# The first loads of a four-layer kernel in five pieces on two queues, with eight small products ahead of them

## The reference, cut to what matters

```
def _dense(x, wi, wo):
    return jax.nn.relu(x @ wi) @ wo
s0 = _dense(hidden_states, share_wi[0], share_wo[0])
...
out = expert_out * g[:, 0, None, None] + s0 * g[:, 1, None, None] + s1 * g[:, 2, None, None] + s2 * g[:, 3, None, None]
```

## Time and profile before

| what | us |
|---|---|
| runs: median of 3 (lowest, highest) | 1641.2 (1638.75, 1642.07) |
| the profiled execution, its own time | 1641.15 |
| its span in the profile | 1639.3 |
| TensorE busy in the span | 1606.8 (98%) |
| TensorE's first matmul starts | 8.78 |
| TensorE's first matmul on `sum` (down 0) starts | 15.02 |

### The profile page before, as it was taken

How to read it: one execution, slowest core, us unless ns; L and a number is a source line. 1 busy time by engine, 2 the same in 40 slices (tenths; PEclk the granted TensorE clock), 3 DMA queues, 4 the chain that set the end, 5 groups by cost and what they waited for, 6 DMA issues and landing times.

```text
span 1639.3 us, 22537 instructions
## 1 busy us (share of the span) xinstructions
PE 1606.8 (98%) x7980; PEld 1360.5 (83%) x7980; DVE 1106.7 (68%) x1710; ACT 861.0 (53%) x1530; POOL 480.7 (29%) x420
## 2 busy tenths in 40 slices
PE   7999999999989999999999999999999999999998
PEld 6898898898977888888888888888888888877887
DVE  5665565465767876776776776776876786666556
ACT  5543343344546666656665665665665665643332
POOL 2121121124733541341431431441440440130000
PEclk9999999999989999999999999999999999999998
DMA  6522131131320010010010010000000010030000
GB/s 207 193 81 75 52 104 51 51 103 52 116 78 26 14 39 27 14 39 26 14 39 26 16 37 27 26 26 26 26 26 26 26 39 14 26 90 17 14 14 26
DMA packets 28460, 79.06 MB, mean 48 GB/s; under 512 B 4790, under 2 KB 9526, under 8 KB 28230
## 3 DMA queue, kind: packets, MB, share of 16 engines
q1 hardware_dynamic: 28054, 76.65, 14.7%
q0 software_dynamic: 304, 1.10, 0.2%
HBM read 75.64 MB, written 2.10 MB: 47 GB/s over the span
## 4 chain that ended last, share of the span: by engine, by line
PE 90%; DVE 6%; issue 2%; ACT 1%; POOL 0%; DMA 0%; POOLq 0%; SPq 0%; ACTq 0%; DVEq 0%
PE sum L396 12%; PE sum L398 12%; PE sum L397 12%; PE up L522 12%; PE up L524 11%; PE up L523 11%; PE up L396 6%; PE up L397 6%; PE up L398 6%; DVE up_tile L1427 2%; DVE x L1415 1%; PE sum L667 0%; DMA raw<-in_shared 0%; DVE gate_tile L1422 0%; PE sum L685 0%
## 5 line engine op out<-in xcount | busy, mean ns | idle before, releaser
L908 ACT ACTIVATE hidden_hi<-up_tile 128x512 fp32r<-128x512 f32 x256 | 161.2, 630 | 190.0 <-DVE up_tile L1427 167.5
L1422 DVE TENSOR_TENSOR gate_tile<-up,gate_tile 128x512 f32<-128x512 f32 x192 | 130.2, 688 | 164.6 <-PE up L524 164.1
L802 ACT ACTIVATE hidden<-up 128x256 fp32r<-128x256 f32 (+1 forms) x224 | 106.3, 475 | 251.6 <-PE sum L398 204.8
L1363 DVE SCALAR_TENSOR_TENSOR hidden<-up,hidden 128x256 fp32r<-128x256 f32 (+1 forms) x224 | 120.3, 537 | 156.7 <-ACT hidden L802 155.3
L1432 DVE TENSOR_TENSOR hidden_lo<-up_tile,hidden_hi 128x512 fp32r<-128x512 f32 x256 | 192.6, 772 | 44.7 <-ACT hidden_hi L908 44.7
L522 PE MATMUL up<-x_sums,gate_up 128*128 128x512 f32 x512 | 201.4, 393 | 3.5 <-ACT gate_tile L897 3.1
L396 PE MATMUL sum<-hidden_hi,down 128*128 128x512 f32 x512 | 199.9, 390 | 3.8 <-DVE gate_exp L1302 3.8
L523 PE MATMUL up<-x_sums,gate_up 128*128 128x512 f32 x512 | 200.8, 392 | 0.0
L524 PE MATMUL up<-x_sums,gate_up 128*128 128x512 f32 x512 | 200.7, 392 | 0.0
L397 PE MATMUL sum<-hidden_lo,down 128*128 128x512 f32 x512 | 199.7, 390 | 0.0
L398 PE MATMUL sum<-hidden_hi,down 128*128 128x512 f32 x512 | 199.7, 390 | 0.0
(11 more groups left out here) (223 smaller groups left out, 3684.2 us busy)
## 6 DMA issues: line engine op xcount, KB each, us to landing
raw<-in_experts SPq DMA_DIRECT2D x64, 512.0 KB, 3.6
raw<-in_l SPq DMA_DIRECT2D x54, 512.0 KB, 3.5
raw<-in_shared SPq DMA_DIRECT2D x12, 512.0 KB, 4.5
raw<-in_xT SPq DMA_DIRECT2D x4, 512.0 KB, 5.7
raw<-in_w SPq DMA_DIRECT2D x8, 256.0 KB, 2.5
out<-out_stage SPq DMA_DIRECT2D x6, 256.0 KB, 2.1
gate_w<-in_gw POOLq DMA_DIRECT2D x1, 1024.0 KB, 7.8
raw<-in_w SPq DMA_DIRECT2D x16, 64.0 KB, 2.4
```

The lines of the kernel that those rows point to most:

```text
L908: A(hi[:, i], cu[:, i], ACT.Copy).then_inc(hi_done, 1)
L1422: V.tensor_tensor(t, ps, t, ALU.add).then_inc(c_done[m], 1)
```

## The change

The first two loads become five. SyncE issues the two halves of x of block 0 (`first_x` for the first, `raw_full[0]` for the second, 256 KB each) and then columns 512 to 1023 of the first weight half (256 KB); ScalarE issues columns 0 to 255 and 256 to 511 (128 KB each) on its own queue, ahead of everything else it does. The high and low parts are made piece by piece, in the order weight piece 0, x group 0, x group 1, then weight pieces 1 and 2, with new semaphores `first_hi` and `first_lo` for three of the five; `w_hi` and `w_lo` reach the same counts as before after the last x piece and the last weight piece. The first step on TensorE waits by piece and takes its six matmuls in another order; the second waits for `first_lo` 3 and the third for `w_lo` 2. Ahead of it all TensorE multiplies `ones` by `ones` eight times (128 columns each, plain float32) into a bank that up 3 overwrites, as soon as `warm` is 1. Nothing that is computed for the output changes but the order in which six partial products are added.

```diff
@@ -200,6 +200,8 @@
 
         raw_full = [sem(f"raw_full{i}") for i in range(RAW)]
         warm = sem("warm")
+        first_x, first_w = sem("first_x"), [sem("first_w0"), sem("first_w1")]
+        first_hi, first_lo = sem("first_hi"), sem("first_lo")
         const_full, gw1_full = sem("const_full"), sem("gw1_full")
         idx_full = sem("idx_full")
         consts = sem("consts")
@@ -291,6 +293,7 @@
             before = sum(1 for bb in range(b) if raw_slot(("plain", PLAIN0 + L1_CH * NE1 + bb)) == raw_slot(key))
             return raw_fill(key) + 32 * (before + 1)
 
+        FIRST = [slice(0, D), slice(D, 2 * D), slice(2 * D, CH)]
         SMALL = 5
         late_small = 3 * B
 
@@ -346,8 +349,13 @@
                         sp.wait_ge(idx_full, 48)
                         t = expert_types(0)
                     load_expert(0, n, t[n // 4], fixed=0)
-                elif n == 0 or n > 4 * NSH:
-                    load_x(0 if n == 0 else n - 4 * NSH, n)
+                elif n == 0:
+                    sp.dma_start(raw[:, 0, 0:BLK], xT_d[:, 0, 0:BLK]).then_inc(first_x, 16)
+                    sp.dma_start(raw[:, 0, BLK:CH], xT_d[:, 1, 0:BLK]).then_inc(raw_full[0], 16)
+                elif n == 1:
+                    sp.dma_start(raw[:, 1, FIRST[2]], sh_d[0][:, FIRST[2]]).then_inc(raw_full[1], 16)
+                elif n > 4 * NSH:
+                    load_x(n - 4 * NSH, n)
                 else:
                     load_plain(n, sh_d[n - 1])
 
@@ -421,17 +429,23 @@
                         pe.wait_ge(exin_lo, q + 1 + tb * EX_CH)
                     wt = lambda hl, dt: exin[:, q % 2, hl, f % 2 * D + dt * P:f % 2 * D + (dt + 1) * P]
                 out = up_ps[:, n % 4, 0:N]
+                if first and n == 1:
+                    pe.wait_ge(first_lo, 3)
+                if first and n == 2:
+                    pe.wait_ge(w_lo, 2)
                 if first and n == 0:
 
+                    pe.wait_ge(first_hi, 2)
+                    pe.matmul(out, wt(0, 0), x_block(tb, 0, half, N, xh), start=True, stop=False)
+                    pe.wait_ge(w_hi, 1)
+                    pe.matmul(out, wt(0, 1), x_block(tb, 1, half, N, xh), start=False, stop=False)
+                    pe.wait_ge(first_lo, 1)
                     for dt in range(DT):
-                        pe.wait_ge(w_hi, 2)
-                        pe.matmul(out, wt(0, dt), x_block(tb, dt, half, N, xh), start=dt == 0, stop=False)
-                    for dt in range(DT):
-                        pe.wait_ge(w_lo, 1)
-                        pe.matmul(out, wt(0, dt), x_block(tb, dt, half, N, xl), start=False, stop=False)
-                    for dt in range(DT):
-                        pe.wait_ge(w_lo, 2)
-                        last = pe.matmul(out, wt(1, dt), x_block(tb, dt, half, N, xh), start=False, stop=dt == DT - 1)
+                        pe.matmul(out, wt(1, dt), x_block(tb, dt, half, N, xh), start=False, stop=False)
+                    pe.wait_ge(first_lo, 2)
+                    pe.matmul(out, wt(0, 0), x_block(tb, 0, half, N, xl), start=False, stop=False)
+                    pe.wait_ge(w_lo, 1)
+                    last = pe.matmul(out, wt(0, 1), x_block(tb, 1, half, N, xl), start=False, stop=True)
                     last.then_inc(up_done, 1)
                     return
                 for dt in range(DT):
@@ -711,6 +725,9 @@
                         last = pe.matmul(out, xl[:, dt, t], w3[b][:, 0, c], start=False, stop=dt == DT - 1)
                 last.then_inc(l3_done, 1)
 
+            pe.wait_ge(warm, 1)
+            for _ in range(8):
+                pe.matmul(up_ps[:, 3, 0:P], ones[:], ones[:], start=True, stop=True)
             l0_block(0, first=True)
             with pe.Fori(1, NB - 1) as tb:
                 l0_block(tb)
@@ -757,7 +774,7 @@
                 plain_hi(o, W[:, 2 * j + r % 2, 0, r // 2 * CH:(r // 2 + 1) * CH])
 
             def x_hi0(o):
-                tb = 0 if o == 0 else o - 4 * NSH
+                tb = o - 4 * NSH
                 plain_hi(o, xh[:, :, tb * BLK:(tb + 1) * BLK])
 
             def expert_hi(ring, part, s, q, tb, loop):
@@ -815,6 +832,8 @@
                         h()
 
 
+            for i in range(2):
+                act.dma_start(raw[:, 1, FIRST[i]], sh_d[0][:, FIRST[i]]).then_inc(first_w[i], 16)
             act.wait_ge(warm, 1)
             A(mhalf[:], mhalf[:], ACT.Copy).then_inc(warm, 1)
 
@@ -823,8 +842,16 @@
                 act.wait_ge(softp, 1)
                 A(gp[:], gp[:], ACT.Exp, scale=10.0).then_inc(softe, 1)
 
-            x_hi0(0)
-            shared_hi(1)
+            act.wait_ge(first_w[0], 16)
+            A(W[:, 0, 0, FIRST[0]], raw[:, 1, FIRST[0]], ACT.Copy).then_inc(first_hi, 1)
+            act.wait_ge(first_x, 16)
+            A(xh[:, 0, 0:BLK], raw[:, 0, 0:BLK], ACT.Copy).then_inc(first_hi, 1)
+            act.wait_ge(raw_full[0], 16)
+            A(xh[:, 1, 0:BLK], raw[:, 0, BLK:CH], ACT.Copy).then_inc(w_hi, 1)
+            act.wait_ge(first_w[1], 16)
+            A(W[:, 0, 0, FIRST[1]], raw[:, 1, FIRST[1]], ACT.Copy).then_inc(first_hi, 1)
+            act.wait_ge(raw_full[1], 16)
+            A(W[:, 0, 0, FIRST[2]], raw[:, 1, FIRST[2]], ACT.Copy).then_inc(w_hi, 1)
             hooks = {n: [lambda o=n + 2: shared_hi(o)] for n in range(6)}
             hooks[6] = [lambda: expert_hi(exin, 0, exin_hi, 0, 0, False), lambda: expert_hi(exout, 1, exout_hi, 0, 0, False)]
             hooks[7] = [lambda: expert_hi(exin, 0, exin_hi, 1, 0, False)]
@@ -1204,8 +1231,8 @@
                 V.tensor_tensor(dst, src, hi.bitcast(f32), ALU.subtract).then_inc(w_lo, 1)
 
             def x_or_shared_lo(o):
-                if o == 0 or o > 4 * NSH:
-                    tb = 0 if o == 0 else o - 4 * NSH
+                if o > 4 * NSH:
+                    tb = o - 4 * NSH
                     sl = slice(tb * BLK, (tb + 1) * BLK)
                     plain_lo(o, xl[:, :, sl], xh[:, :, sl])
                 else:
@@ -1242,8 +1269,16 @@
 
             V.memset(ones[:], 1.0)
             V.memset(mhalf[:], -0.5).then_inc(warm, 1)
-            x_or_shared_lo(0)
-            x_or_shared_lo(1)
+            def first_lo_part(done, n, dst, src, hi, out):
+
+                dve.wait_ge(done, n)
+                V.tensor_tensor(dst, src, hi.bitcast(f32), ALU.subtract).then_inc(out, 1)
+
+            first_lo_part(first_hi, 1, W[:, 0, 1, FIRST[0]], raw[:, 1, FIRST[0]], W[:, 0, 0, FIRST[0]], first_lo)
+            first_lo_part(first_hi, 2, xl[:, 0, 0:BLK], raw[:, 0, 0:BLK], xh[:, 0, 0:BLK], first_lo)
+            first_lo_part(w_hi, 1, xl[:, 1, 0:BLK], raw[:, 0, BLK:CH], xh[:, 1, 0:BLK], w_lo)
+            first_lo_part(first_hi, 3, W[:, 0, 1, FIRST[1]], raw[:, 1, FIRST[1]], W[:, 0, 0, FIRST[1]], first_lo)
+            first_lo_part(w_hi, 2, W[:, 0, 1, FIRST[2]], raw[:, 1, FIRST[2]], W[:, 0, 0, FIRST[2]], w_lo)
 
             def l0_take(tb, jj):
```

## The result

The changed kernel took 1635.72 us (median of 7 runs, 1634.21 to 1636.87), the kernel before beside it 1640.82 (7 runs, 1638.75 to 1642.07). The ratio is 0.9969, interval 0.9959 to 0.9979: 5.1 us faster, by the interval 3.4 to 6.7. The profiled execution took 1636.87 with a span of 1635.0, so the spans of the two profiles differ by 4.3 us. The forecast was 1639.6, a gain of 1.6 us, and its range ended at 1637.5: the direction was right, the gain three times as large.

What follows compares the result with a forecast made beforehand. TensorE's wait for the first data and its low clock after it were taken to bound the start. Earlier landing 1.90 us less 0.26 for the clock gave 1.64; 1641.2 - 1.6 = 1639.6 us, range 1637.5 to 1641.8.

Steps and rivals of the forecast that it cites:

- What bounds the start: TensorE's first matmul waits until 8.78 for 1 MB and two activations, then runs without a gap to down 0.
- When the pieces land: First loads: same byte curve, new order; second x half lands at 6.8, matmul 2 at 7.45, up 1 1.90 us earlier.
- The issue was called hidden: SyncE's issues of the pieces cost nothing: even three of 0.71 us in a row end at 2.9.
- The rule: Queues share 16 DMA engines and interleave: second x half lands at 7.0, gain 1.4 us instead of 1.6.
- my half-way value: Second x half's landing taken at 6.8, the middle of 6.6 to 7.0, only half way to the interleaving rule.
- High and low parts: Piecewise conversions: ScalarE 0.62 us for 512 columns, 0.38 for 256; VectorE 0.69 and 0.42.
- The products of ones: Eight on TensorE before the data: 3.5 us, ending at about 4.6, no cost; no clock gain counted.
- The cap: Down 0 needs the third load's low part, chained to the first `hidden`: no more than about 2.15 us won.
- rival A: Clock already high when the second x half comes: up 1 at 8.6, 3.2 us won, 1638.0; chance 15%.
- B: Second x half lands only with the whole megabyte at 7.67: 0.8 us won, 1640.4; chance 14%.
- C: Small packets hold the pieces at 75 GB/s, second x half lands at 10.2: slower, 1642.9; chance 5%.
- my slow clock: Up 0 and up 1 at 0.43 us per matmul; slow stretch again 4.4 us from matmul 2, costing 0.26 us.

Runs made afterwards that it cites:

- x_halves: Kernel before with only x of block 0 issued as two 256 KB transfers, its high part still behind both; single executions 1643.5 and 1640.0 us.
- one_queue: Changed kernel with all five pieces issued by SyncE on one queue, second x half ahead of weight pieces 1 and 2; 1636.2 us, ratio 0.9968.
- before_ones16: Kernel before with only 16 products of ones added; 1640.8 us, one execution.
- late_small: Kernel before with GpSimd's five small constants issued only after x's low part, their vector work three steps later; 1638.1 us, one execution.
- before_ones24: Kernel before with only 24 products of ones added, reaching up to the first data; 1639.3 us, ratio 0.9989.
- no_ones: Changed kernel without the eight products of ones; 1637.4 us, ratio 0.9976.
- two_queues_whole: Kernel before with the whole first weight half issued by ScalarE on its own queue beside SyncE's whole x; 1640.6 us, one execution.
- before_ones8: Kernel before with only the eight products of ones added; 1640.4 us, ratio 0.9995.

## Why the prediction was wrong, point by point

- **What bounds the start** was right: TensorE ran without a gap from the first matmul, and what was won by down 0 reached the end. The down 0 of the changed kernel is 4.16 us earlier, and the interval of the time holds that.
- **When the pieces land** failed first. "The total does not change, only its order" took the curve of bytes of the earlier trace rows as given. It began to rise 0.3 to 0.6 us sooner, and then it had no trough: 655 to 786 kB were moved at 4.5 to 5.0, not 5.55 to 5.9. The second x half was there by 5.47 instead of 6.8, and matmul 2 started at 6.16 instead of 7.45: 1.3 us. x_halves shows such a curve with only x split. Some 0.9 to 1.0 us of the 1.3 are the curve. The rest is the step from the bytes moved to the engine: the prediction took 1.05 us, and here it was 0.5 to 0.9 (5.47 less 4.5 to 5.0); in one_queue, where the order is plain, 131, 393 and 655 kB were moved at about 2.4, 3.5 and 4.7 and taken at 3.09, 4.20 and 5.51, 0.7 to 0.8 us later. Why the trough goes stays open.
- **The issue was called hidden**, "an issue that nothing is waiting for". The first transfer itself waits for its own issue: it takes 0.40 us instead of 0.71, and the first bytes move before 1.8 instead of after 2.1. This is a smaller part of the miss than it looks, since by 3.0 both kernels had moved nearly the same (229 and 221 kB).
- **The second queue.** The rule and my half-way value differed by 0.2 us; one_queue put matmul 2 at 6.19 against 6.16, less than either. It moves the third load by 0.7 us, which the sum did not have.
- **High and low parts** were right to 0.04 us: 0.42, 0.61 and 0.63 on ScalarE.
- **The products of ones** were costed right (end at 4.84, forecast 4.6, no cost) and their effect wrong. The step that failed was "I take no gain from them". Adding 24 alone gives 1.24 us of down 0; taking the eight out of the changed kernel costs 0.74 to 1.25 from matmul 2 on. The step rested on the late landing: with 1.4 and 1.0 us of idle behind the products it looked open; the idle was 0.7 us, and even 2.5 us (before_ones16) were harmless. Rows of before left the low stretch at 2.7 to 6.0 us, and 3.8 us of products were enough in four profiles of four.
- **The cap** was right in kind, and as a figure it was not one: "no more than about 2.15 us can be won" was said "whatever the clock does", and 4.16 were won. It hung on the first `hidden`, and that moves with up 0 and so with the clock, as the prediction's own rival A has it. In the changed kernel down 0 does wait 0.5 us for the low part of the third load, where the forecast had no new wait up to 460, and the load itself, "there before ScalarE wants it", now was what ScalarE waited for (0.16 us, up to 8.40).
- **Rivals.** A was what happened: high clock, up 1 with its low part just there, a wait ahead of down 0. It was priced at 3.2 us on my landings; the landing adds 1.0. B and C, both on late landings, were out. C read the trough as the work of the small packets, which late_small shows they are in part at most.
- **The two misses together**: forecast 1.64, measured 4.16 at down 0. With the measured landing and my slow clock the sum would have been 1.64 + 1.29 = 2.93; the remaining 1.23 is the clock, and before_ones24 measures 1.24 for it. no_ones, the changed kernel at the slow clock, has 15.02 - 12.24 = 2.8, but that it comes so near 2.93 is in part luck: its matmul 2 was 0.64 us later, and its clock rose 3.2 us after matmul 2 instead of the supposed 4.4, which gives 0.6 back (1.2 x 0.47). By down 0 either alone would have stayed below 0.2% (3.3 us); the forecast itself had no case in which both came, and A had only one of them.

## What to carry to other kernels

At a cold start, cost the first transfer from the end of its own issue, and let the piece that the first matmul needs be a short transfer of its own, even where everything goes through one queue. Fill TensorE's wait for the first data with cheap products that reach up to within a microsecond or two of the data; half as many, or the same number with 3.7 us of idle behind, gave nothing that the time showed. Take the landings of a changed order of loads from a trace and not from the old curve of bytes. Compare two executions from the same event on (here matmul 2), or a landing that differs by chance is counted as an effect. Then look for what is needed next: here the third load became the wait, and its first quarter was all that was needed.

## What was not expected of the hardware

- Splitting a 512 KB load into two of 256 KB, same bytes and order, brought x's landing forward from 5.9 us (four profiles) to 5.25 and 5.41, and the next load's from 7.45 to 7.82 to 6.97 in both. Only about 0.3 us of this is the shorter first issue (0.40 for 0.71 us).
- What an issue costs here went with the rows and not with the bytes: 512 KB of x in 256 rows of 2 KB took 0.71 us, 256 KB in 128 rows 0.40 to 0.42, 128 KB in 128 rows 0.40 to 0.46, and 512 KB of weights in 128 rows of 4 KB 0.39 on ScalarE's queue (two_queues_whole) and 0.33 to 0.58 on SyncE's.
- A trough between about 3.9 and 5.1 us in all profiles that begin with one whole 512 KB load of x on one queue (lowest slice 75 to 130 GB/s), with a second queue beside it shifted to 4.5 to 6.0 (212 down to 137), and absent, shorter or earlier where x was split. Its cause is open.
- Two whole loads of 512 KB issued at the same time on two queues landed 2.4 us apart (4.4 and 6.8): the one in 128 rows well ahead of the one in 256.
- The clock kept its high level over 2.5 us of idle and lost it over 3.7 us, one profile each. From the first real matmul at the low level to the rise it took 3.3 to 5.9 us in eight profiles, with the same work behind it.
- The granted clock in the profile prints 1.00 through a low stretch that stands at the very start (first line); only the spacing of the matmuls shows it. Once the clock has been high the print is right: before_ones8 prints 0.50 from 8.75 on.
